# Eight adds of 128 spread through the statistics, in place of two adds of 512

## The chip, the core and the metric

The kernel runs on one core of one Trainium2 chip. A core has five engines that run their own instruction streams and meet only at semaphores: TensorE (PE, matmul and transpose; its weight loads are shown as PEld), VectorE (DVE), ScalarE (ACT), GpSimd (POOL) and SyncE (SP, which here only issues DMA). The metric is the device time of one execution in microseconds (us); lower is better.

## What is computed

One pre-normalised layer of a graph network: N = 50000 nodes of 128 features, E = 25000 edges with 32 features, all float32. The edges come sorted by their end node `dst`.

```python
h = jnp.maximum(_layernorm(x, axis=-1), 0.0)
src = edge_index[0]
dst = edge_index[1]
msg_input = jnp.concatenate([h[src], h[dst], edge_attr], axis=-1)
x = jax.nn.relu(msg_input @ Wm1 + bm1)
messages = jax.nn.relu(x @ Wm2 + bm2)
agg = jax.ops.segment_sum(messages, dst, num_segments=N)
update_input = jnp.concatenate([h, agg], axis=-1)
u = jax.nn.relu(update_input @ Wu1 + bu1)
h_new = h + (u @ Wu2 + bu2)
...
x = x + h_new
```

## The kernel before

The program has two parts with a barrier between them. Part one (to about 683 us in the profile) is a loop of 49 rounds, one for each block of 512 edges and 1024 nodes. Part two adds the messages up by node and makes the output. The change is in part one, in VectorE's program (`vector_1`).

A tile is 128 rows by 128 features. In round s part one takes 8 tiles of edge ends (4 of `x[src]`, 4 of `x[dst]`), gathered by GpSimd into `xg`, and 8 tiles of nodes, loaded into `xn` by a DMA that ScalarE issues. It forms the normalised edge ends, sends them through the two message layers, and leaves the messages in `msgs`. From the nodes it forms W_uh h + b_u1 (part of the update's first layer, `hu`) and x + h + b_out (`xh`). Both go to scratch in DRAM (`hu_scratch`, `xh_scratch`, 512 KB a round each), and part two reads them back.

The rounds are software-pipelined. Body s of VectorE does, in this order:

- waits until `xn` of round s has landed (L387), then the sixteen-column arithmetic of the layer norm of round s-1 (`statistics`, L312 to L355): `pair`, `diff`, `sq`, `mean`, `var`, `veps`, then, once ScalarE has made the square root `sd`, the reciprocal, a Newton step (r1, r2), `rstd` and `shift`. Each of these small instructions waits on a semaphore for the one before, and in the gaps `between(i)` puts independent work: `bn_stats` of node tile i of round s for i = 0 to 7 (L304), `x_plus_h` for i = 8 and 9 (L360, 512 wide: max(zn, 0) + xn of round s-2 into `xh_o`), `add_b_out` for i = 10 and 11 (L366, 512 wide);
- `normalise` of round s-1 (L378): the 8 tiles of `xg` in place, and one node tile into `zn`. ScalarE makes the other seven node tiles (L429) as soon as `shift` is there;
- waits for the gather of round s (L307) and takes `bn_stats` of its 8 tiles (L309).

ScalarE's round is, in program order: `sd` (L453); the bias eviction of the second W_uh product of round s-3 (L441); the first message layer's ReLU (L458); the bias eviction of the first W_uh product of round s-2 (L441, it waits for TensorE's L511); three `zn` tiles, which wait for `shift`; the issue of the two scratch stores of round s-3 (L447 `hu`, L449 `xh`); the second message layer's ReLU (L467); four `zn` tiles; the ReLU evictions of transposed groups 0 and 1 (L436); the issue of the load of `xn` and `edge` of round s+1 (L174, L181); the message eviction (L478); the evictions of groups 2 and 3, which also wait until both stores of this round have landed (L483). The stores and the loads share ScalarE's DMA queue and stand in it in that order.

TensorE's round is: W_uh product 0, second message layer, W_uh product 1, transposes of group 0 and 1 (the `xg` tiles, L504), message products (L534), transposes of groups 2 and 3 (`zn`), first message layer of the next round (L520 to L522).

GpSimd only gathers: it copies eight columns of indices, waits until the gather before has landed (L239), and issues eight indirect DMAs (L246). A slot of `xg` is free again three rounds later (L236).

`x_plus_h` and `add_b_out` count in `s_xs` and `s_xh`, each twice a round. Before it writes `xh_o`, VectorE waits that ScalarE and it itself have made `zn` of that round (`s_za`, `s_zv`), and that the stores that read this half of `xh_o` two rounds ago have landed (`s_sto`, L396).

Of the kernel before, what the change touches and what calls it, by code (L numbers as in the profile page):

```python
# [10 lines left out]
ALU = mybir.AluOpType  # L11
# [4 lines left out]
N, E, D, DE = 50000, 25000, 128, 32  # L16
# [26 lines left out]
def at_least(s, k):  # L43

    return not isinstance(s, int) or s >= k


def below(s, k):

    return not isinstance(s, int) or s < k  # L50


def build(nc, x, ends, dst_rows, dst_cols, edge_t, wm1, bm1, wm2, bm2, wu1, bu1, wu2, bu2, out):
    with ExitStack() as ctx:
        def sb(name, shape, dt=F32, on=ctx):
            return on.enter_context(nc.sbuf_tensor(name, shape, dt))
# [4 lines left out]
        def sem(name):  # L61
            return ctx.enter_context(nc.semaphore(name))
# [21 lines left out]
        xh_o = sb("xh_o", [P, 2, 2, W])  # L84
# [15 lines left out]
        s_xs, s_xh = sem("x_and_h_summed"), sem("xh_ready")  # L100
# [32 lines left out]
        with ExitStack() as one:  # L133
# [14 lines left out]
            xn = sb("xn", [P, 4, 8, D], on=one)  # L148
            zn = sb("zn", [P, 2, 8, D], on=one)
# [141 lines left out]
            def vector_1(dve):  # L291
# [20 lines left out]
                def statistics(s, slot, between):  # L312


                    half = slot % 2
                    if at_least(s, 2):
                        dve.wait_ge(s_za, 2 * (s - 1))
                        dve.wait_ge(s_zv, 3 * (s - 1))
                    dve.wait_ge(s_stat, STAT * s + 1)
                    dve.tensor_tensor(pair[:], bn[:, half, :, 1:3], bn[:, half, :, 4:6], ALU.add).then_inc(s_stat, 1)  # L320
                    dve.tensor_tensor(diff[:], bn[:, half, :, 1], bn[:, half, :, 4], ALU.subtract).then_inc(s_stat, 1)
                    between(0)
                    dve.wait_ge(s_stat, STAT * s + 3)
                    dve.scalar_tensor_tensor(out=sq[:], in0=diff[:], scalar=0.25, in1=diff[:], op0=ALU.mult,
                                             op1=ALU.mult).then_inc(s_stat, 1)
                    dve.tensor_scalar(mean[:, half], pair[:, :, 0], 0.5, None, ALU.mult).then_inc(s_stat, 1)
                    between(1)
                    dve.wait_ge(s_stat, STAT * s + 5)
                    dve.scalar_tensor_tensor(out=var[:], in0=pair[:, :, 1], scalar=1.0 / D, in1=sq[:], op0=ALU.mult,
                                             op1=ALU.add).then_inc(s_stat, 1)  # L330
                    between(2)
                    dve.wait_ge(s_stat, STAT * s + 6)
                    dve.tensor_scalar(veps[:], var[:], EPS, None, ALU.add).then_inc(s_stat, 1)  # L333
                    for i in range(3, 6):
                        between(i)
                    dve.wait_ge(s_sd, s + 1)
                    dve.reciprocal(r0[:], sd[:]).then_inc(s_stat, 1)
                    between(6)
                    dve.wait_ge(s_stat, STAT * s + 8)

                    dve.scalar_tensor_tensor(out=r1[:], in0=r0[:], scalar=-0.5, in1=r0[:], op0=ALU.mult,
                                             op1=ALU.mult).then_inc(s_stat, 1)
                    between(7)
                    dve.wait_ge(s_stat, STAT * s + 9)
                    dve.tensor_tensor(r2[:], r1[:], veps[:], ALU.mult).then_inc(s_stat, 1)
                    between(8)
                    dve.wait_ge(s_stat, STAT * s + 10)
                    dve.scalar_tensor_tensor(out=rstd[:, half], in0=r2[:], scalar=1.5, in1=r0[:], op0=ALU.add,  # L348
                                             op1=ALU.mult).then_inc(s_stat, 1)
                    between(9)  # L350
                    dve.wait_ge(s_stat, STAT * s + 11)
                    dve.scalar_tensor_tensor(out=shift[:, half], in0=mean[:, half], scalar=-1.0, in1=rstd[:, half], op0=ALU.mult,
                                             op1=ALU.mult).then_inc(s_stat, 1)
                    between(10)
                    between(11)  # L355

                def x_plus_h(s, slot, h):

                    half = slot % 2
                    dve.scalar_tensor_tensor(  # L360
                        out=xh_o[:, half, h, :].rearrange("p (j d) -> p j d", j=4), in0=zn[:, half, 4 * h:4 * h + 4, :],
                        scalar=0.0, in1=xn[:, slot, 4 * h:4 * h + 4, :], op0=ALU.max, op1=ALU.add).then_inc(s_xs, 1)

                def add_b_out(s, slot, h):
                    dve.wait_ge(s_xs, 2 * s + h + 1)
                    dve.tensor_tensor(xh_o[:, slot % 2, h, :], xh_o[:, slot % 2, h, :], b_out[:], ALU.add  # L366
                                      ).then_inc(s_xh, 1)
# [15 lines left out]
                def body(s, slot, use):  # L383
                    prev, prev2 = (slot - 1) % 4, (slot - 2) % 4
                    if below(s, STEPS):

                        dve.wait_ge(s_xn[slot], 32 * use + 32 + (0 if below(s, STEPS - 1) else 16))  # L387
                    def between(i):
                        if i < 8 and below(s, STEPS):
                            stat_of_nodes(s, slot, i)  # L390
                        if i == 8 and at_least(s, 2):
                            dve.wait_ge(s_za, 2 * (s - 1))
                            dve.wait_ge(s_zv, 3 * (s - 1))
                            if at_least(s, 4):

                                dve.wait_ge(s_sto[slot % 2], 64 * use + (32 if slot >= 2 else 0) - 32)  # L396
                        if i in (8, 9) and at_least(s, 2):
                            x_plus_h(s - 2, prev2, i - 8)
                        if i >= 10 and at_least(s, 2):
                            if not at_least(s, 3):  # L400
                                dve.wait_ge(s_w, 16 * 11)
                            add_b_out(s - 2, prev2, i - 10)

                    if at_least(s, 1) and below(s, STEPS + 1):
                        statistics(s - 1, prev, between)
                        normalise(s - 1, prev)
                    else:
                        for i in range(12):
                            between(i)
                    if not at_least(s, 1):  # L410
                        finish_table(dve, did)
                        assert steps[0] == TABLE
                    if below(s, STEPS):
                        stat_of_ends(s, slot, use)

                run_steps(dve, STEPS + 2, 4, STEPS - 1, 4, body)

            def scalar_1(act):
# [441 lines left out]
```

## Time and profile before

| | us |
|---|---|
| median of 3 runs | 946.89 |
| lowest, highest | 946.84, 947.41 |
| the profiled execution | 952.33 |
| its span on the core | 950.6 |

The rows further down come from that one profiled execution; its span is the time from its first to its last recorded instruction. In a timeline row the first number is the start, the second the time that the instruction (or the row of merged instructions, xN) is busy, and the bracket tells how long the engine sat idle before it and what released it. Instructions on VectorE and ScalarE overlap in their pipelines, so the distance between two starts is shorter than a row's busy time.

### The profile page before, as it was taken

To read this page: it belongs to the slowest core of one execution; us is meant where nothing else is said; L and a number is where in the kernel's file an instruction comes from. 1 tells how busy PE (TensorE), PEld (TensorE's weight loads), DVE (VectorE), ACT (ScalarE), POOL (GpSimd) and SP (SyncE) were. 2 spreads that over 40 slices of the span, in tenths; PEclk is the share of its full clock that TensorE was granted. 3 is DMA by queue.
4 is the path that set the end of the run, shared out by engine and by line. 5 is a ranking of instruction groups with operands and counts; after the bars stand their busy time and mean duration, and the time that the engine had idled before them with its cause. 6 is when DMAs were issued, how large, how long until landed. Compare 5 with 4: busy or idle time off the path is not lost. (4 is left out here: it accounts for less than half of the span.)

```text
span 950.6 us, 19507 instructions
## 1 busy us (share of the span) xinstructions
PE 751.0 (79%) x3158; PEld 453.1 (48%) x3159; DVE 696.0 (73%) x2407; ACT 608.5 (64%) x1384; POOL 566.0 (60%) x829
## 2 busy tenths in 40 slices
PE   0687768767877778877887776886799999999998
PEld 0344334333433334433443433453457788777776
DVE  3866756666677666776667567766499999998887
ACT  0666556556656565665665566655567788988986
POOL 6656655656566555665556555654198766655453
PEclk9988888889789897889887899988899999999999
DMA  6254445445545455545553454447305799999999
GB/s 158 67 178 158 151 154 175 157 127 178 176 157 168 141 176 165 169 148 161 177 176 129 153 176 155 162 150 232 133 12 176 230 319 335 351 341 349 355 360 328
DMA packets 99726, 184.55 MB, mean 194 GB/s; under 512 B 15101, under 2 KB 16512, under 8 KB 99700
## 3 DMA queue, kind: packets, MB, share of 16 engines
q1 hardware_dynamic: 46084, 80.64, 25.4%
q10 hardware_dynamic: 41072, 77.93, 23.5%
q0 software_dynamic: 12544, 25.72, 10.5%
q14 instruction: 20, 0.16, 0.1%
q8 instruction: 6, 0.10, 0.0%
HBM read 107.25 MB, written 76.98 MB: 194 GB/s over the span
## 5 line engine op out<-in xcount | busy, mean ns | idle before, releaser
L246 POOL DMA_INDIRECT xg<-x_in,ends_now x392 | 386.1, 985 | 142.9 <-issue 130.1
L511 PE MATMUL bank<-ht,w_uh 128*128 128x512 f32 x196 | 146.1, 837 | 114.2 <-ACT ht L441 68.8
L644 POOL TENSOR_TENSOR low<-msgs,high 128x128 fp32r<-128x128 f32 x303 | 152.8, 521 | 73.3 <-ACT high L724 70.1
L309 DVE BATCH_NORM_STATS2 bn<-xg 128x6 f32<-128x128 f32 x392 | 80.6, 278 | 132.4 <-DMA xg<-x_in,ends_now 132.3
L673 DVE TENSOR_SCALAR hot<-node,dst_f,minus_base 128x512 fp32r<-128x512 f32 x229 | 131.2, 616 | 23.2 <-issue 16.3
L777 PE MATMUL bank<-hot,low 128*128 128x512 f32 x303 | 136.4, 450 | 12.2 <-POOL low L644 6.5
L429 ACT ACTIVATE zn<-xn,shift,rstd 128x128 f32<-128x128 f32 x343 | 141.6, 483 | 1.6 <-DVE rstd L348 1.2
L511 PEld LDWEIGHTS bank<-ht,w_uh 128*128 128x128 f32 x196 | 42.6, 249 | 199.6 <-issue 180.1
L436 ACT ACTIVATE ht<-bank 128x512 f32<-128x512 f32 x196 | 109.2, 593 | 30.3 <-PE bank L504 26.1
L778 PE MATMUL bank<-hot,high 128*128 128x512 f32 x303 | 120.8, 399 | 0.0
L504 PE MATMUL bank<-ident,xg 128*128 128x128 f32 x392 | 64.8, 298 | 61.1 <-issue 37.0
L378 DVE TENSOR_SCALAR xg<-xg,mean,rstd 128x128 f32<-128x128 f32 x392 | 106.3, 352 | 0.0
L811 PEld LDWEIGHTS bank<-w_out,u_t 128*128 128x128 f32 x784 | 99.3, 191 | 14.2 <-issue 8.0
L811 PE MATMUL bank<-w_out,u_t 128*128 128x128 f32 x784 | 105.1, 277 | 0.2 <-ACT u_t L757 0.2
L441 ACT ACTIVATE ht<-bank,b_u 128x512 f32<-128x512 f32 x98 | 66.6, 680 | 58.5 <-issue 31.5
L504 PEld LDWEIGHTS bank<-ident,xg 128*128 128x128 f32 x392 | 49.0, 154 | 109.5 <-issue 90.7
L724 ACT ACTIVATE high<-msgs 128x128 fp32r x303 | 81.7, 298 | 28.6 <-issue 16.8
L304 DVE BATCH_NORM_STATS2 bn<-xn 128x6 f32<-128x128 f32 x392 | 98.3, 276 | 0.0
L453 ACT ACTIVATE sd<-veps 128x16 f32<-128x16 f32 x49 | 10.6, 216 | 125.6 <-DVE veps L333 102.8
L777 PEld LDWEIGHTS bank<-hot,low 128*128 128x128 f32 x303 | 57.9, 191 | 52.3 <-issue 25.3
L243 POOL COPY ends_now<-ends_all 128x8 int32 (+1 forms) x45 | 8.4, 187 | 115.5 <-DMA xg<-x_in,ends_now 56.8
L527 PE MATMUL bank<-m1t,w_msg 128*128 128x512 f32 x98 | 76.2, 873 | 0.0
(77 smaller groups left out, 1165.7 us busy)
## 6 DMA issues: line engine op xcount, KB each, us to landing
hu_scratch<-ht ACTq DMA_DIRECT2D x49, 512.0 KB
xh_scratch<-xh_o ACTq DMA_DIRECT2D x49, 512.0 KB
hu_i<-hu_scratch SPq DMA_DIRECT2D x98, 256.0 KB
xh_i<-xh_scratch SPq DMA_DIRECT2D x98, 256.0 KB
out<-xh_o SPq DMA_DIRECT2D x97, 256.0 KB, 4.3
xn<-x_in ACTq DMA_DIRECT2D x44, 512.0 KB
xg<-x_in,ends_now POOLq DMA_INDIRECT x392
edge<-edge_t_in ACTq DMA_DIRECT2D x45, 64.0 KB
```

What stands on the lines that cost most here:

```text
L246: pool.indirect_dma_start(xg[:, slot, t, :], None, x, bass.IndirectOffsetOnAxis(ap=ends_now[:, slot8, t:t + 1], axis=0)).then_inc(s_xg[slo ...
L304: dve.bn_stats(bn[:, slot % 2, 8 + t, :], xn[:, slot, t, :])
L378: ins = dve.tensor_scalar(to, of, mean[:, slot % 2, t:t + 1], rstd[:, slot % 2, t:t + 1], ALU.subtract, ALU.mult)
L429: ins = act.activation(zn[:, prev % 2, t - 8, :], xn[:, prev, t - 8, :], ACT.Identity, bias=shift[:, prev % 2, t:t + 1], scale=rstd[:, pre ...
L436: act.activation(ht[:, prev % 2, q, :], p_tr[q][:], ACT.Relu).then_inc(s_ht, 1)
L504: ins = pe.transpose(p_tr[q][:, j * P:(j + 1) * P], of, ident[:])
L511: pe.matmul(p_hu[:], w_uh[:], ht[:, slot % 2, 2 + n, :], start=True, stop=True).then_inc(s_hus, 1)
L644: return pool.tensor_tensor(low[:, at, :], msgs[:, k, :], high[:, at, :].bitcast(F32), ALU.subtract)
L673: return dve.tensor_scalar(hot[:, at, :], node[:], dst_f[:, bass.ds(k, 1)], minus_base[:, bass.ds(g, 1)], ALU.subtract, ALU.is_equal)
L777: pe.matmul(to, low[:, at, :], hot[:, at, :], start=start, stop=False, skip_group_check=True)
L778: return pe.matmul(to, high[:, at, :], hot[:, at, :], start=False, stop=stop, skip_group_check=True)
L811: ins = pe.matmul(to[:, j * D:(j + 1) * D], u_t[:, slot % 2, j * P:(j + 1) * P], w_out[:], start=True, stop=True)
```

## The change

`x_plus_h` is cut from two instructions of 512 columns a round to eight of 128, one behind each `bn_stats` of the node tiles. The three waits ahead of it move with it, from before position 8 to position 0. Only the fourth and the eighth of the eight add one to `s_xs`, so that there are still two increments a round. `add_b_out` stays 512 wide and moves from positions 10 and 11, behind `shift`, to positions 8 and 9: one between r2 and `rstd`, one between `rstd` and `shift`.

```diff
                     dve.scalar_tensor_tensor(out=shift[:, half], in0=mean[:, half], scalar=-1.0, in1=rstd[:, half], op0=ALU.mult,
                                              op1=ALU.mult).then_inc(s_stat, 1)
-                    between(10)
-                    between(11)
-
-                def x_plus_h(s, slot, h):
-
-                    half = slot % 2
-                    dve.scalar_tensor_tensor(
-                        out=xh_o[:, half, h, :].rearrange("p (j d) -> p j d", j=4), in0=zn[:, half, 4 * h:4 * h + 4, :],
-                        scalar=0.0, in1=xn[:, slot, 4 * h:4 * h + 4, :], op0=ALU.max, op1=ALU.add).then_inc(s_xs, 1)
+
+                def x_plus_h(s, slot, t):
+
+                    ins = dve.scalar_tensor_tensor(
+                        out=xh_o[:, slot % 2, t // 4, t % 4 * D:(t % 4 + 1) * D], in0=zn[:, slot % 2, t, :],
+                        scalar=0.0, in1=xn[:, slot, t, :], op0=ALU.max, op1=ALU.add)
+                    if t % 4 == 3:
+                        ins.then_inc(s_xs, 1)
...
-                        if i == 8 and at_least(s, 2):
+                        if i == 0 and at_least(s, 2):
                             dve.wait_ge(s_za, 2 * (s - 1))
                             dve.wait_ge(s_zv, 3 * (s - 1))
                             if at_least(s, 4):
 
                                 dve.wait_ge(s_sto[slot % 2], 64 * use + (32 if slot >= 2 else 0) - 32)
+                        if i < 8 and at_least(s, 2):
+                            x_plus_h(s - 2, prev2, i)
                         if i in (8, 9) and at_least(s, 2):
-                            x_plus_h(s - 2, prev2, i - 8)
-                        if i >= 10 and at_least(s, 2):
                             if not at_least(s, 3):
                                 dve.wait_ge(s_w, 16 * 11)
-                            add_b_out(s - 2, prev2, i - 10)
+                            add_b_out(s - 2, prev2, i - 8)
```

On VectorE, in a round ahead of the loop, between `var` and the reciprocal (L337). `sd` is made by ScalarE from `veps`. Before:

```order
L329 SCALAR_TENSOR_TENSOR var<-pair,sq 128x16
L304 BN_STATS bn<-xn 128x6
L333 TENSOR_SCALAR veps<-var 128x16
L304 BN_STATS bn<-xn 128x6 x3
L337 RECIPROCAL r<-sd 128x16
```

And now:

```order
L329 SCALAR_TENSOR_TENSOR var<-pair,sq 128x16
L304 BN_STATS bn<-xn 128x6
L357 SCALAR_TENSOR_TENSOR xh_o<-zn,xn 128x128
L333 TENSOR_SCALAR veps<-var 128x16
L304 BN_STATS bn<-xn 128x6
L357 SCALAR_TENSOR_TENSOR xh_o<-zn,xn 128x128
L304 BN_STATS bn<-xn 128x6
L357 SCALAR_TENSOR_TENSOR xh_o<-zn,xn 128x128
L304 BN_STATS bn<-xn 128x6
L357 SCALAR_TENSOR_TENSOR xh_o<-zn,xn 128x128
L337 RECIPROCAL r<-sd 128x16
```

One narrow add stands behind each `bn_stats`; three of the eight are ahead of `veps`, three more ahead of the reciprocal.

On VectorE, in the same round, from the last Newton product (`r<-r,veps`) to the normalisation of the gathered tiles. Before:

```order
L345 TENSOR_TENSOR r<-r,veps 128x16
L360 SCALAR_TENSOR_TENSOR xh_o<-zn,xn 128x512
L348 SCALAR_TENSOR_TENSOR rstd<-r 128x16
L360 SCALAR_TENSOR_TENSOR xh_o<-zn,xn 128x512
L352 SCALAR_TENSOR_TENSOR shift<-mean,rstd 128x16
L366 TENSOR_TENSOR xh_o<-xh_o,b_out 128x512 x2
L378 TENSOR_SCALAR xg<-xg,mean,rstd 128x128 x8
```

And now:

```order
L345 TENSOR_TENSOR r<-r,veps 128x16
L365 TENSOR_TENSOR xh_o<-xh_o,b_out 128x512
L348 SCALAR_TENSOR_TENSOR rstd<-r 128x16
L365 TENSOR_TENSOR xh_o<-xh_o,b_out 128x512
L352 SCALAR_TENSOR_TENSOR shift<-mean,rstd 128x16
L377 TENSOR_SCALAR xg<-xg,mean,rstd 128x128 x8
L377 TENSOR_SCALAR zn<-xn,mean,rstd 128x128
```

The two wide adds of `b_out` took the places of the two wide `x_plus_h`, so that nothing stands between `shift` and the normalisation any more. No other engine's order is changed.

## Rows read from the trace of the kernel before

**Rows 1.** Waits by engine and line, 100 to 640 us: total, times, longest.
```profile
DVE bn L309 <- DMA xg<-x_in,ends_now: 115.3, 40, 5.8
...
DVE pair L320 <- DMA edge<-edge_t_in: 58.0, 33, 2.6
```

**Rows 2.** Timeline of VectorE: `pair` that opens body 3 and, 44 rounds later, body 47.
```profile
45.15 0.20 DVE L320 TENSOR_TENSOR pair<-bn 128x32 f32<-128x32 f32 x1
...
637.07 0.20 DVE L320 TENSOR_TENSOR pair<-bn 128x32 f32<-128x32 f32 x1 [1.99 <-DMA edge<-edge_t_in]
```

**Rows 3.** Timeline of VectorE, one round, 301.31 to 315.00 us, and the next one's end.
```profile
301.31 0.19 DVE L320 TENSOR_TENSOR pair<-bn 128x32 f32<-128x32 f32 x1 [1.39 <-DMA edge<-edge_t_in]
...
301.72 0.16 DVE L324 SCALAR_TENSOR_TENSOR sq<-diff 128x16 f32<-128x16 f32 x1
301.81 0.16 DVE L326 TENSOR_SCALAR mean<-pair 128x16 f32<-128x16 f32 x1
...
302.43 0.66 DVE L304 BATCH_NORM_STATS2 bn<-xn 128x6 f32<-128x128 f32 x3
...
303.76 0.69 DVE L360 SCALAR_TENSOR_TENSOR xh_o<-zn,xn 128x512 f32<-128x512 f32 x1
...
305.06 0.17 DVE L352 SCALAR_TENSOR_TENSOR shift<-mean,rstd 128x16 f32<-128x16 f32 x1
...
306.35 2.13 DVE L378 TENSOR_SCALAR xg<-xg,mean,rstd 128x128 f32<-128x128 f32 x8
...
310.89 1.64 DVE L309 BATCH_NORM_STATS2 bn<-xg 128x6 f32<-128x128 f32 x8 [2.15 <-DMA xg<-x_in,ends_now]
315.00 0.20 DVE L320 TENSOR_TENSOR pair<-bn 128x32 f32<-128x32 f32 x1 [2.46 <-DMA edge<-edge_t_in]
...
328.04 0.20 DVE L320 TENSOR_TENSOR pair<-bn 128x32 f32<-128x32 f32 x1 [1.58 <-DMA edge<-edge_t_in]
```

**Rows 4.** Timeline of ScalarE and its DMA issues (ACTq), the same round and the next.
```profile
305.31 0.48 ACT L429 ACTIVATE zn<-xn,shift,rstd 128x128 f32<-128x128 f32 x1
...
305.95 0.42 ACTq L449 DMA_DIRECT2D xh_scratch<-xh_o  x1
...
310.50 0.60 ACT L436 ACTIVATE ht<-bank 128x512 f32<-128x512 f32 x1 [1.35 <-PE bank L504]
310.73 0.40 ACTq L174 DMA_DIRECT2D xn<-x_in  x1
...
319.83 0.48 ACT L429 ACTIVATE zn<-xn,shift,rstd 128x128 f32<-128x128 f32 x1
320.20 0.42 ACTq L449 DMA_DIRECT2D xh_scratch<-xh_o  x1
...
324.05 0.40 ACTq L174 DMA_DIRECT2D xn<-x_in  x1
```

**Rows 5.** Timeline of TensorE, the transposes of group 1 in that round.
```profile
308.54 0.66 PE L504 MATMUL bank<-ident,xg 128*128 128x128 f32 x4 [0.30 <-issue]
```

**Rows 6.** Stretches: engines' busy us, granted clock (PEclk), DMA share, GB/s.
```profile
305.95:310.30 4.35, 3.12 (x22) 2.18 (x21) 2.79 (x10) 3.20 (x8) 2.74 (x3) 1.00 0.90 300
315.00:320.00 5.00, 2.84 (x4) 1.17 (x4) 4.98 (x23) 2.12 (x5) 3.78 (x5) 0.55 0.20 54
```

**Rows 7.** Timeline of GpSimd, the copies that open two of its rounds.
```profile
311.09 0.19 POOL L243 COPY ends_now<-ends_all 128x8 int32 x1 [1.79 <-PE bank L504]
...
325.04 0.19 POOL L243 COPY ends_now<-ends_all 128x8 int32 x1 [3.44 <-DMA xg<-x_in,ends_now]
```

**Rows 8.** Timeline, a round with a late gather, from its `pair`.
```profile
111.67 0.20 DVE L320 TENSOR_TENSOR pair<-bn 128x32 f32<-128x32 f32 x1 [0.17 <-DVE bn L309]
...
116.76 0.42 ACTq L449 DMA_DIRECT2D xh_scratch<-xh_o  x1
...
119.89 0.40 ACTq L174 DMA_DIRECT2D xn<-x_in  x1
...
125.00 1.64 DVE L309 BATCH_NORM_STATS2 bn<-xg 128x6 f32<-128x128 f32 x8 [5.82 <-DMA xg<-x_in,ends_now]
```

More of the change, by code:

```diff
@@ L407, in body @@
                     else:
-                        for i in range(12):
+                        for i in range(10):
                             between(i)
```

## The prediction

> **What bounds the kernel now.** I read the waits first: VectorE waits in every round for the gathered tiles (115.3 us in 40 waits between 100 and 640 us) and in most again, at `pair`, for the load of the nodes (58.0 us in 33) [rows 1]. A total does not say which of the two sets the pace, so I read rounds in the timeline. From `pair` at 45.15 to `pair` at 637.07 there are 44 rounds of 13.45 us on average [rows 2]. In the round from 301.31 the gather lands at 310.89, its statistics take 1.64 us, and VectorE then sits 2.46 us until the load is there, at 315.00 [rows 3]. The wait that ends last is the one for the load; the gather has over 2 us of slack. So one round is a ring: `pair`, statistics, normalisation, transposes, eviction of group 1, issue of the next load (L174, 9.42 us after `pair`), its landing (4.27 us), next `pair`: 13.69 us. The next round has 9.05 and 3.99 us, 13.04 in all [rows 3, 4].
>
> Two kinds of round alternate irregularly. In the round from 301.31 the granted clock is 1.00 (2.4 GHz) from the stores' issue to their end. In the first 5 us of the next it is 0.55 on average, mostly the lower level of 1.2 GHz [rows 6], TensorE's W_uh products take longer there, and the first `zn` follows `pair` by 4.83 us in place of 4.00 [rows 3, 4]. About half of the rounds are of each kind.
>
> GpSimd has a ring of its own: copy, eight gathers, landing, copy. Between two copies lie 13.95 us, 3.44 of them idle; with the 1.79 us of idle that another round has, it would be 12.3 us [rows 7]. It is the faster ring, by about 1 us. In five of 47 rounds it nevertheless decides: the load is issued 3.13 us after the stores (4.78 in the round above), the gather lands only at 125.00, 13.33 us after `pair`, and with its statistics of 1.64 the round takes 15.0 us [rows 3, 4, 8].
>
> **The narrow add.** Only starts count, since instructions overlap. A 16-column instruction of this kind takes 0.09 us (`sq` to `mean`). The 512-column one takes 0.61: from 303.76 to 305.06 there are two and one `rstd`, (1.30 - 0.09)/2. A line through both gives 0.09 + 0.52 x 112/496 = 0.207 us at 128 columns, and eight `bn_stats` of 128 columns in a row take 1.64 us, 0.205 each [rows 3]. Eight take 1.65 us in place of 1.21: **+0.44 us** a round. The other end is 0.27 us, that of a tile of the `xg` normalisation with its two column operands (2.13/8) [rows 3]: +0.92. I take 0.207, as both nearest rows agree. No gap of the statistics chain is there to swallow it: from `pair` to `shift`, 3.75 us, VectorE's rows carry no idle time in brackets [rows 3]. So the interleaving hides nothing; below zero is excluded.
>
> One rule speaks for a higher price. Three narrow instructions in a row are recorded as 0.66 us together, and a wide one as 0.69 though the next wide one follows it closely [rows 3]: they overlap. The Trainium skill (VectorE: DVE Perf Modes, the section on the TRN2 errata) says that the latency is exposed between instructions, so that many small tiles pay it each time, and gives (N+151)/0.96 for an fp32 add; by that, as an estimate, eight of 128 take 2.33 us and two of 512 1.38, +0.95 a round, in place of +0.44. The trace agrees with its duration of 0.69 for one of 512 columns, not with paying it in full between instructions.
>
> **The moved adds of b_out.** Their two 0.6 us are spent either way (from `shift` at 305.06 to the normalisation at 306.35: 1.29, less 0.09, is 1.20 for two) [rows 3]. But they now come ahead of `shift`. `shift` moves from 3.75 us after `pair` to 3.75 + 0.44 + 1.20 = 5.39. Three paths lead from `pair` to the issue of the load:
> - VectorE's own: the normalisation of `xg`, from which group 1 is transposed, starts 0.44 later. In rounds at full clock this path decides: ScalarE waits 1.35 us for group 1 [rows 4]. **+0.44**.
> - `veps` and `sd`: three narrow adds now stand ahead of `veps`, 0.62 us. `sd` and all that ScalarE does behind it, the evictions that TensorE's W_uh products wait for among them, come 0.6 later. In rounds at low clock TensorE reaches the transposes late by this path. **+0.6**.
> - ScalarE's `zn` tiles: they start 0.25 us behind `shift` (305.06 to 305.31), so at 5.6 us, where they were at 4.0 and 4.83. From the first to the issue of the load are 4.22 us in the round with little waiting (319.83 to 324.05) [rows 3, 4]; 5.6 + 4.2 = 9.8, against 9.42 + 0.44 = 9.86 and 9.05 + 0.6 = 9.65. So this path becomes level with the others and adds 0 to 0.15. I take 0.
>
> The mean of 0.44 and 0.60 is +0.52 a round.
>
> **The stores.** They are issued behind the third `zn`, 4.64 and 5.20 us after `pair` (L449); 0.64 behind the first `zn`, they go to about 6.25 [rows 3, 4]. They keep the DMA 0.90 busy for 4.35 us [rows 6], now until 10.6 us. The load, issued at 9.8 behind them in the same queue, has 3.55 us from the stores' issue in place of 4.78 and 3.85. With 3.85 it landed as fast (3.99 us) as with 4.78 (4.27), with 3.13 the round was late by the gather [rows 4, 8]. The load's landing thus costs 0 to 0.8 us more (its queue ahead ends 0.8 after its issue); I take 0, the distance being nearer to 3.85. But late rounds become more frequent: each costs 15.0 - 13.3 = 1.7 us, and I count two more, **+3 us** in all.
>
> **The waits that move.** `s_za` and `s_zv` were satisfied in the round before. `s_sto` asks for the stores of the round before, and VectorE has just waited for a load that stands behind them in the queue; it can bind only in the last body, where no load is waited for, and there the same two stages of work stand behind it as before. Two increments a round stay two. Part two is untouched.
>
> **Sum.** 47 rounds end in a wait for a load, 47 x 0.52 = 24.4 us; the two bodies behind them have only VectorE's 0.44 each, 0.9; late rounds 3. Together +28 us on the profiled 952.33, which is 980.6, or 1.030. On the median of 946.89 that is **975 us**. With 0.44 everywhere and no late rounds it is 967; with 0.6 + 0.15 a round and four late ones 990.
>
> **Rivals.**
> - *Absorbed.* If the gathers really set the pace, VectorE's longer work only shortens its 2.15 us wait for them: 947. For it: that wait is the larger total [rows 1]. Against: the wait for the load follows it and ends last in most rounds [rows 3].
> - *Faster.* The five late rounds vanish because the slower main ring leaves the gather ring more slack, while the +0.44 hides in the 1.35 us for which group 1's signal is late: its transposes are recorded at 308.54 for 0.66 us, yet ScalarE gets it at 310.50 [rows 4, 5]. Then 5 x 1.6 = 8 us are gained: 939. It decides once the signal does not move with VectorE. Against: low-clock rounds show no such gap.
> - *Stores, gathers and load collide in most rounds.* The load now follows the stores at 3.55 us, between the 3.13 of a late round and 3.85. If half of the rounds take 15 us [rows 8], the mean gains (15.0 - 13.3)/2 = 0.85, and the other half keeps its share of 0.52, 0.26; together +1.11, 47 x 1.11 = 52: 999.
> - *The late signal belongs to the store burst.* Group 1's signal at 310.50 coincides with the end of the burst at 310.30 [rows 4, 6]. If the burst holds it, the load moves by as much as the stores, 1.6 and 1.05 us: 47 x 1.3 = 61: 1008.
> - *The narrow adds cost +0.92* (their upper end): 0.96 or so a round with the rest, 45 + 3: 995. The skill's page named above gives nearly the same price.
>
> **Chances.** Forecast 0.58; absorbed 0.10; faster 0.07; collisions 0.15; burst 0.06; dear adds 0.04. The two rivals below my forecast are the 0.17 that I leave out, with part of the burst case: range 957 to 1000. A measurement of this kernel tells about 0.2% from no change: faster by more 0.08, within it 0.09, slower 0.83.
>
> **What would show it.** Right: narrow adds start about 0.2 us apart; `shift` at 5.4 us behind `pair`; the first L428 `zn` at 5.6 and the stores' issue at 6.2; the load's issue at 9.7 to 9.9, landing about 4 us later; mean round 14.0. VectorE's wait at `pair` for the load stays or grows, that for the gather shrinks by less than 0.5. Wrong: a round that stays at 13.4 (the gathers' ring), a load issue near 11 us (the burst), or rounds of 15 with waits of over 5 us for the gather in more than a fourth of all (collisions).

## The result and the profile after

The changed kernel takes 980.52 us (median of 4 runs, 977.82 to 985.02) against 947.15 (4 runs). The ratio is 1.0356, with a 95% interval of 1.0316 to 1.0395: slower, by 33 us where 28 were forecast. The profiled execution has a span of 978.4 us, 950.6 before: 28 us more and not 33, since the profiled execution of the kernel before (952.33) is itself 5 us above the median. These 28 us all lie in part one: from the third body's `pair` on, 42 rounds take 14.15 us each in place of 13.47.

VectorE's timeline of the changed kernel, `pair` of body 3 and, 42 rounds later, of body 45 (start, busy us, engine, line, operation; in brackets the idle time before it and its releaser), which answers to [rows 2]:

```profile
44.47 0.20 DVE L320 TENSOR_TENSOR pair<-bn 128x32 f32<-128x32 f32 x1
...
638.78 0.20 DVE L320 TENSOR_TENSOR pair<-bn 128x32 f32<-128x32 f32 x1 [4.35 <-DMA edge<-edge_t_in]
```

Its waits between 100 and 640 us (total, times, longest), which answer to [rows 1]:

```profile
DVE pair L320 <- DMA edge<-edge_t_in: 174.6, 38, 5.3
...
ACT msgs L477 <- remote: 100.0, 35, 4.2
...
DVE bn L309 <- DMA xg<-x_in,ends_now: 2.7, 1, 2.7
```

VectorE waits no longer for the gathers (115.3 us before, 2.7 now) and three times as long for the load (58.0 before, 174.6 now). That the load's ring sets the pace was right; but the gathers now have a lead: they have landed before VectorE asks for them, which no step of mine foresaw.

One round on VectorE, beside [rows 3]:

```profile
314.95 0.20 DVE L320 TENSOR_TENSOR pair<-bn 128x32 f32<-128x32 f32 x1 [4.89 <-DMA edge<-edge_t_in]
...
316.19 0.29 DVE L304 BATCH_NORM_STATS2 bn<-xn 128x6 f32<-128x128 f32 x1
316.40 0.28 DVE L357 SCALAR_TENSOR_TENSOR xh_o<-zn,xn 128x128 f32<-128x128 f32 x1
316.59 0.17 DVE L333 TENSOR_SCALAR veps<-var 128x16 f32<-128x16 f32 x1
...
320.21 0.17 DVE L352 SCALAR_TENSOR_TENSOR shift<-mean,rstd 128x16 f32<-128x16 f32 x1
...
322.65 1.64 DVE L309 BATCH_NORM_STATS2 bn<-xg 128x6 f32<-128x128 f32 x8
328.84 0.20 DVE L320 TENSOR_TENSOR pair<-bn 128x32 f32<-128x32 f32 x1 [4.56 <-DMA edge<-edge_t_in]
```

A narrow add takes 0.19 us from its start to the next (0.207 forecast). `shift` stands 5.26 us behind `pair` (5.39 forecast, 3.75 before). The statistics of the gathered tiles follow the normalisation with no wait at all, and 4.56 us of idle time come at the end.

ScalarE in the same round, beside [rows 4]:

```profile
316.79 0.21 ACT L452 ACTIVATE sd<-veps 128x16 f32<-128x16 f32 x1 [1.66 <-DVE veps L333]
...
320.41 0.49 ACT L428 ACTIVATE zn<-xn,shift,rstd 128x128 f32<-128x128 f32 x1
...
321.10 0.43 ACTq L448 DMA_DIRECT2D xh_scratch<-xh_o  x1
...
324.48 0.40 ACTq L174 DMA_DIRECT2D xn<-x_in  x1
...
327.76 0.60 ACT L477 ACTIVATE msgs<-bank 128x512 f32 x1 [2.85 <-remote]
```

The first `zn` starts 5.46 us after `pair` and the stores are issued at 6.15 (5.6 and 6.25 forecast). The load is issued at 9.53 in this round and at 9.08 on average. That is no later than before (9.14), where 9.7 to 9.9 was forecast. It lands 4.36 us later here and 5.07 on average, against 4.33 before. So the issue did not move; the landing did.

Why the issue did not move shows on ScalarE. Before, it idled ahead of the evictions of the transposed groups (waits from 100 to 640 us, the kernel before):

```profile
ACT ht L436 <- PE bank L504: 23.1, 31, 1.9
```

Over the 42 rounds that is 0.59 us a round ahead of groups 0 and 1. In the changed kernel it is 0.05: VectorE's later work and the later `zn` tiles went into a wait that had been there. And from the first `zn` to the load's issue are 3.51 us on average (5.57 to 9.08), where 4.22 was forecast. A round at full clock of the changed kernel, its `pair` at 582.48:

```profile
587.94 0.49 ACT L428 ACTIVATE zn<-xn,shift,rstd 128x128 f32<-128x128 f32 x1 [0.86 <-DVE shift L352]
...
588.63 0.42 ACTq L448 DMA_DIRECT2D xh_scratch<-xh_o  x1
...
590.93 0.40 ACTq L174 DMA_DIRECT2D xn<-x_in  x1
```

Here the load is issued 8.45 us after `pair`, over 1 us earlier than in the round from 314.95, with the stores at the same 6.15. The round is no shorter for it: 13.85 us against 13.89.

The share of the DMA engines fits this. Stretches of 1 us of the kernel before, the round of [rows 3] (busy us of the engines, granted clock, DMA share, GB/s):

```profile
308.31:309.31 1.00, 0.77 (x7) 0.77 (x8) 0.43 (x2) 0.84 (x2) 0.98 (x1) 1.00 1.02 356
309.31:310.31 1.00, 1.00 (x11) 1.00 (x11) 0.00 (x0) 0.00 (x0) 0.00 (x0) 1.00 0.71 189
310.31:311.31 1.00, 0.81 (x7) 0.58 (x6) 0.42 (x3) 0.60 (x1) 0.19 (x1) 1.00 0.02 4
311.31:312.31 1.00, 1.00 (x3) 0.52 (x4) 1.00 (x7) 0.52 (x2) 0.54 (x1) 1.00 0.44 68
312.31:313.31 1.00, 1.00 (x3) 0.24 (x2) 0.23 (x2) 1.00 (x3) 0.70 (x2) 1.00 0.97 342
```

And of the changed kernel, from its stores on:

```profile
321.95:322.95 1.00, 1.00 (x2) 0.23 (x1) 1.00 (x5) 1.00 (x4) 0.69 (x2) 0.50 1.02 350
322.95:323.95 1.00, 1.00 (x9) 0.97 (x8) 1.00 (x6) 0.98 (x4) 0.69 (x2) 0.78 1.04 402
323.95:324.95 1.00, 1.00 (x11) 1.00 (x10) 0.33 (x2) 0.96 (x2) 0.90 (x1) 1.00 0.97 301
324.95:325.95 1.00, 1.00 (x11) 1.00 (x10) 0.00 (x0) 0.00 (x0) 0.79 (x1) 1.00 0.78 113
325.95:326.95 1.00, 1.00 (x4) 0.45 (x3) 0.00 (x0) 0.00 (x0) 0.16 (x1) 1.00 0.71 258
326.95:327.95 1.00, 1.00 (x3) 0.29 (x2) 0.00 (x0) 0.19 (x1) 0.00 (x0) 1.00 1.00 377
```

Before, the DMA engines fall idle (0.02) between the stores and the load: the load waits for its issue. Now stores, gathered rows (the second at 0.78 and only 113 GB/s) and load follow each other without a gap: the load waits for what is ahead of it. Its landing follows the stores' issue, 7.7 us earlier in this round and 7.9 on average (14.15 - 6.25), and no longer its own. The rounds of the timeline agree: in the 41 that end in this wait, the load lands the slower the closer it is issued behind the `xh` store (slope -0.96, correlation -0.89). In 34 such rounds of the kernel before the slope is 0.04.

### The profile page after: what moved, and what is told of

It reads as the page before. It is cut to its first block and busy times, and to the rows that moved or that the text cites. A ratio compares the mean times of both kernels' runs of the same rounds, so it can differ in the third digit from the quotient of the medians.

```text
span 978.4 us, 19801 instructions
## 1 busy us (share of the span) xinstructions
PE 766.3 (78%) x3158; PEld 459.7 (47%) x3159; DVE 710.2 (73%) x2701; ACT 608.0 (62%) x1384; POOL 572.0 (58%) x829
## 5 line engine op out<-in xcount | busy, mean ns | idle before, releaser
L510 PE MATMUL bank<-ht,w_uh 128*128 128x512 f32 x196 | 164.0, 933 | 158.0 <-ACT ht L440 143.1
L510 PEld LDWEIGHTS bank<-ht,w_uh 128*128 128x128 f32 x196 | 48.4, 275 | 247.3 <-issue 196.8
L320 DVE TENSOR_TENSOR pair<-bn 128x32 f32<-128x32 f32 x49 | 9.6, 196 | 197.6 <-DMA edge<-edge_t_in 192.2
L304 DVE BATCH_NORM_STATS2 bn<-xn 128x6 f32<-128x128 f32 x392 | 108.2, 278 | 0.0
L357 DVE SCALAR_TENSOR_TENSOR xh_o<-zn,xn 128x128 f32<-128x128 f32 x392 | 105.6, 271 | 3.4 <-DMA xh_scratch<-xh_o 3.4
L477 ACT ACTIVATE msgs<-bank 128x512 f32 (+1 forms) x49 | 29.2, 597 | 113.0 <-remote 107.0
L503 PEld LDWEIGHTS bank<-ident,xg 128*128 128x128 f32 x392 | 52.2, 158 | 82.3 <-issue 77.6
L503 PE MATMUL bank<-ident,xg 128*128 128x128 f32 x392 | 59.6, 294 | 35.1 <-issue 30.2
L526 PE MATMUL bank<-m1t,w_msg 128*128 128x512 f32 x98 | 86.7, 985 | 0.0
```

Source lines behind the costliest of these rows:

```text
L304: dve.bn_stats(bn[:, slot % 2, 8 + t, :], xn[:, slot, t, :])
L503: ins = pe.transpose(p_tr[q][:, j * P:(j + 1) * P], of, ident[:])
L510: pe.matmul(p_hu[:], w_uh[:], ht[:, slot % 2, 2 + n, :], start=True, stop=True).then_inc(s_hus, 1)
```

## The experiments

I formed two theories from this. The **path theory** is my prediction's: the round grows because the narrow adds and `sd` make the load's issue late. The **store theory**: `shift` holds the first `zn` tiles, behind them the stores, and the load lands about 8 us behind the stores' issue. The table gives, for each kernel, the ratio to the kernel before on the same chip with its 95% interval, and means over the same 42 rounds of the profiled execution, taken from the timelines' rows: the round, `shift`, the issue of the `xh` store and of the load (us after `pair`), and VectorE's wait for the gathers. Each mean is of one execution: that of the kernel before is 0.6% above its median, that of "before, stores early" 0.6% below (933.61 against 939.0), so differences of 0.1 us between rounds say nothing, and the ratios decide.

| kernel | ratio (95%) | round | shift | stores | load | gather wait |
|---|---|---|---|---|---|---|
| before | 1 | 13.47 | 3.79 | 4.99 | 9.14 | 2.95 |
| changed | 1.0356 (1.0316 to 1.0395) | 14.15 | 5.33 | 6.25 | 9.08 | 0.36 |
| only narrowed | 1.0046 (1.002 to 1.0072) | 13.52 | 4.29 | 5.34 | 8.98 | 0.30 |
| adds behind shift | 1.0183 (1.0132 to 1.0233) | 13.74 | 4.40 | 5.69 | 9.33 | 0.19 |
| narrow adds behind root | 1.0345 (1.0279 to 1.0411) | 14.22 | 5.42 | 6.33 | 8.87 | 0.18 |
| before, stores late | 1.0311 (1.0228 to 1.0395) | 14.13 | 3.79 | 6.11 | 9.30 | 4.25 |
| changed, stores ahead of zn | 1.0195 (1.0149 to 1.0241) | 13.69 | 5.42 | 5.45 | 9.31 | 0.22 |
| changed, loads by SyncE | 1.0277 (1.0205 to 1.0350) | 13.72 | 5.28 | 6.17 | 9.54 | 3.33 |
| changed, stores early | 1.0271 (1.0221 to 1.0320) | 13.85 | 5.38 | 3.42 | 9.51 | 0.06 |
| before, stores early | 0.9970 (0.9941 to 1.0000) | 13.12 | 3.80 | 2.76 | 8.93 | 0.46 |
| wide adds ahead of shift | 1.0605 (1.0558 to 1.0652) | 14.62 | 4.87 | 5.78 | 8.70 | 5.22 |
| before, load at head | 0.9698 (0.9656 to 0.9740) | 12.59 | 3.77 | 4.83 | (11.47) | 3.45 |
| changed, load at head | 0.9864 (0.9814 to 0.9914) | 13.05 | 5.27 | 6.18 | (11.65) | 3.60 |
| before, load at head, stores early | 0.9663 (0.9623 to 0.9703) | 12.65 | 3.78 | 2.80 | (11.65) | 3.51 |

(In brackets: with the load at the head of ScalarE's body, the issue that falls into the round is that of a load which is needed only a round later.)

### Only narrowed

```diff
                         if i in (8, 9) and at_least(s, 2):
-                            x_plus_h(s - 2, prev2, i - 8)
+                            for t in range(4 * (i - 8), 4 * (i - 8) + 4):
+                                x_plus_h(s - 2, prev2, t)
```

> The kernel before with nothing but the narrowing: four narrow adds at each of the two old places (8 and 9), b_out behind shift. The disputed cost by itself. VectorE takes 0.44 us more a round, shift comes at 4.2, the first zn at 4.4 (full clock) or 4.85 (low), the stores' issue at 5.1 to 5.2. Path theory: 47 x 0.44 = 21 us, 968. Store theory: the stores are later by 0.4 in full-clock rounds alone and not late enough to bind (5.2 + 8.0 = 13.2), so only what VectorE's path gives in full-clock rounds: 950 to 962.

1.0046, some 4 us. It is clear of no change but far from 21 us. `shift` came at 4.29, half a microsecond later than before (0.44 forecast), and the stores at 5.34. This kernel's gathers run ahead too (its wait for them is 0.30 us a round), so the few late rounds of [rows 8] are gone, and part of the price may be paid back by that; this was not separated.

### The two moved parts, each without the other

The adds of `b_out` back behind `shift`, the narrow ones spread as in the change:

```diff
-                        if i in (8, 9) and at_least(s, 2):
+                        if i >= 10 and at_least(s, 2):
...
-                            add_b_out(s - 2, prev2, i - 8)
+                            add_b_out(s - 2, prev2, i - 10)
```

> The changed kernel with the two wide adds of b_out back behind shift; the eight narrow adds stay spread through the statistics. Store theory (the load lands about 8 us after the stores' issue, because it queues behind them): shift goes back to about 4.1 us after pair, but sd is still 0.6 late, so in rounds at low clock the first zn and the stores' issue stay at 5.45 and 6.15 and only the rounds at full clock get their stores at about 5.3; mean round 13.8 to 14.0, 965 to 975 us. Path theory (my prediction's: VectorE's own path and sd's path to the load's issue): the moved adds cost nothing by themselves, so as the changed kernel, 978 to 983. If shift alone is what delays the stores: near 955.

All narrow adds behind the reciprocal, the adds of `b_out` ahead of `shift`:

```diff
-                        if i == 0 and at_least(s, 2):
+                        if i == 6 and at_least(s, 2):
...
-                        if i < 8 and at_least(s, 2):
-                            x_plus_h(s - 2, prev2, i)
+                        if i in (6, 7) and at_least(s, 2):
+                            for t in range(4 * (i - 6), 4 * (i - 6) + 4):
+                                x_plus_h(s - 2, prev2, t)
```

> The changed kernel with all eight narrow adds behind the reciprocal (four at position 6, four at 7), so that veps and sd are as early as in the kernel before; the adds of b_out stay ahead of shift, at 5.3 us after pair. Store theory: first zn at 5.5 and stores' issue at 6.15 in every round, since shift alone holds them: as the changed kernel, mean round 14.1, 976 to 983. Path theory: the 0.6 us of the low-clock rounds is gone and only VectorE's 0.44 is left: 965 to 970.

With `shift` early and `sd` late: 1.0183, 13.74 us a round (963 us, just under what the store theory gave). With `shift` late and `sd` early: 1.0345, the whole loss, 14.22. Beside the narrowing alone (1.0046), spreading the adds ahead of `sd` costs 1.4% and moving the `b_out` adds ahead of `shift` 3.0%; together they cost 3.1%, not 4.4%. They don't add up because the first `zn` starts at the later of two events: at 4.79 us on average with the narrowing alone, 5.29 and 5.63 in these two, 5.57 in the changed kernel. There both stand at the same time: the eviction of the W_uh product, late by `sd`, lets it start at 5.46 in rounds at the low clock, and `shift` lets it start at 5.46 in the others. The path theory, which made `sd` half of the loss and the `b_out` adds free, is refuted in this: 965 to 970 was expected of the second kernel and 979 to 982 came.

### Stores late, VectorE untouched

```diff
-                    if at_least(s, 3):
-                        store(s - 3, (slot + 1) % 2)
...
                         normalise(range(12, 16))
+                    if at_least(s, 3):
+                        store(s - 3, (slot + 1) % 2)
```

> The kernel before, VectorE untouched, with ScalarE's two stores issued behind the second four zn in place of the first three: their issue goes from 4.6 to 5.2 to about 7.3 to 8.1 us after pair, and nothing that makes the load's issue late is touched. Store theory: the load lands 8 us behind the stores' issue, rounds of 15.3 to 16: 1030 to 1065. Path theory: the load's issue at 9.2 and its landing in 4.0 are unchanged, up to 0.8 more for the queue: 947 to 985.

Nothing on VectorE differs from the kernel before and the load's issue hardly moves (9.30), yet the round is 14.13 us and the ratio 1.0311. The direction is the store theory's, and the size is near the loss of the change. The size I had expected (1030 us and more) was wrong for one reason first: ScalarE's queue issues DMAs while the `zn` tiles ahead of them still run, so the stores went out at 6.11 on average and not at 7.3 to 8.1. One of its rounds, VectorE and ScalarE's issues:

```profile
256.99 0.19 DVE L320 TENSOR_TENSOR pair<-bn 128x32 f32<-128x32 f32 x1 [0.91 <-DMA edge<-edge_t_in]
...
268.68 1.64 DVE L309 BATCH_NORM_STATS2 bn<-xg 128x6 f32<-128x128 f32 x8 [4.27 <-DMA xg<-x_in,ends_now]
270.70 0.20 DVE L320 TENSOR_TENSOR pair<-bn 128x32 f32<-128x32 f32 x1 [0.38 <-DMA edge<-edge_t_in]
```

```profile
263.64 0.42 ACTq L449 DMA_DIRECT2D xh_scratch<-xh_o  x1
...
266.34 0.40 ACTq L174 DMA_DIRECT2D xn<-x_in  x1
```

Stores at 6.65, load at 9.35, landing at 13.71, only 7.1 us behind the stores; the gather lands 11.69 us after `pair`, close ahead of the load. In other rounds of this kernel the gather is the later of the two (VectorE waits 4.25 us a round for it). So later stores alone, with VectorE untouched, bring a loss of that size; they hold both the load and the gathers, and 8 us is no constant.

### Taking the stores out of the way of the changed kernel

Three ways. Ahead of the `zn` tiles, so that they don't wait for `shift`:

```diff
+                    if at_least(s, 3):
+                        store(s - 3, (slot + 1) % 2)
                     if has_norm:
                         act.wait_ge(s_stat, STAT * (s - 1) + 12)
                         normalise(range(VECTOR_TILES, 12))
-                    if at_least(s, 3):
-                        store(s - 3, (slot + 1) % 2)
```

> The changed kernel with ScalarE's two stores issued ahead of the first zn tiles, so that they no longer stand behind the wait for shift; VectorE as changed. Store theory: the stores' issue comes back to 4.5 (full clock) or 5.3 (low), mean round 13.4 to 13.6, 945 to 958. Path theory: the load's issue is late by VectorE and sd as before and the stores don't matter: 975 to 981.

Right behind the eviction that they need:

```diff
                         w_h(s - 3, (slot - 3) % 2, 1)
+                        store(s - 3, (slot + 1) % 2)
```

> The changed kernel with the stores issued right behind the eviction of W_uh product 1, so at about 3.3 us after pair whatever shift does. Store theory: all that is left of the change is VectorE's 0.44 and sd's 0.6 on the way to the load's issue; a ratio of 0.997 (the kernel before with early stores) to 1.015. Path theory: the ratio stays at 1.03 and above.

And the load through SyncE's queue, at the same point of the round:

```diff
+                def ahead(s, slot, use):
+                    if below(s, STEPS - 1) and at_least(s, 3):
+                        sp.wait_ge(s_ht, 4 * (s - 1) + 1)
+                        sp.wait_ge(s_tr, 4 * (s - 1) + 2)
+                        sp.wait_ge(s_xh, 2 * (s - 2))
+                        sp.wait_ge(s_m1, s - 2)
+                        load_nodes(sp, s + 1, (slot + 1) % 4)
...
-                    if below(s, STEPS - 1) and at_least(s, 3):
-                        act.wait_ge(s_xh, 2 * (s - 2))
-                        act.wait_ge(s_m1, s - 2)
-                        load_nodes(act, s + 1, (slot + 1) % 4)
```

> The changed kernel with the load of xn and edge issued by SyncE instead of ScalarE, at the same point of the round (group 0 evicted, group 1 transposed), so through another DMA queue. If the load is late because it stands behind the stores in one queue: it now shares the DMA engines with them and lands about 4 us after its issue at 9, mean round 13.3 to 13.7, 945 to 960. If the DMA engines' total work behind the stores (1 MB of stores, the gathers' rows, 0.5 MB of load) sets it and not the queue's order: 975 to 985.

They give 1.0195, 1.0271 and 1.0277, rounds of 13.69, 13.85 and 13.72 us. The last two don't differ clearly from each other, and SyncE's interval overlaps the change's. The three edits thus take back 0.8 to 1.6% of 3.6; none is back at the kernel before, as the store theory wanted, and the last two stay near the 3% of the path theory. What the stores cost the change can be more than was taken back, for the two moved issues bring waits of their own: ahead of the `zn` tiles they hold the first of these to 6.16 us (5.57 in the changed kernel), and early they hold the first layer's ReLU, 44.1 us in 38 waits:

```profile
ACT m1t L458 <- issue: 44.1, 38, 1.3
```

Through SyncE's queue the load is issued at 9.54 and lands 4.2 us later, not 5.07. That speaks for its place behind the stores in one queue, but the gathers have no lead in that kernel, so it is no clean comparison.

In the kernel with early stores the load no longer lands late, and the way to its issue is what is left. A round of it:

```profile
285.35 0.20 DVE L320 TENSOR_TENSOR pair<-bn 128x32 f32<-128x32 f32 x1 [4.48 <-DMA edge<-edge_t_in]
...
290.62 0.18 DVE L352 SCALAR_TENSOR_TENSOR shift<-mean,rstd 128x16 f32<-128x16 f32 x1
...
298.71 0.19 DVE L320 TENSOR_TENSOR pair<-bn 128x32 f32<-128x32 f32 x1 [4.00 <-DMA edge<-edge_t_in]
```

```profile
288.66 0.42 ACTq L448 DMA_DIRECT2D xh_scratch<-xh_o  x1
290.84 1.26 ACT L428 ACTIVATE zn<-xn,shift,rstd 128x128 f32<-128x128 f32 x3 [0.44 <-DVE shift L352]
...
294.57 0.40 ACTq L174 DMA_DIRECT2D xn<-x_in  x1
```

The stores are out at 3.31, ScalarE waits for `shift`, the load is issued at 9.22 and lands 4.14 us later. That kernel's partner is the kernel before with the same edit, whose first ReLU waits as long (48.8 us in 42 waits):

> The kernel before with the stores issued right behind the eviction of W_uh product 1 that they need, about 2 us after pair instead of 4.6 to 5.2. Store theory: the burst is over at 7, group 1's signal isn't held by it, the load is issued at 8.2 to 9 and lands in 4: rounds of 12.4 to 13.0, 897 to 926. Path theory: nothing on the path moves, 940 to 950.

It is at 0.9970, rounds of 13.12 and a load issue at 8.93. Early stores alone bring the kernel before hardly anything: the 12.4 to 13.0 that the store theory gave was missed. And between the two kernels with early stores the change costs 1.0271/0.9970 = 1.030, its load issue going from 8.93 to 9.51, +0.58 us (+0.46 without the first five rounds, in four of which `shift` came up to 1.5 us late). There the path theory has the size (+0.52 forecast). It has not the way: ScalarE waits only 0.05 us a round for the transposes, which leaves ScalarE's own tiles behind `shift`, the path that I had priced at nothing.

### The adds of b_out ahead of shift, nothing narrowed

```diff
-                    between(10)
-                    between(11)
...
-                        if i in (8, 9) and at_least(s, 2):
-                            x_plus_h(s - 2, prev2, i - 8)
-                        if i >= 10 and at_least(s, 2):
+                        if i in (6, 7) and at_least(s, 2):
+                            x_plus_h(s - 2, prev2, i - 6)
+                        if i in (8, 9) and at_least(s, 2):
```

> The kernel before without any narrowing: the two wide x_plus_h at positions 6 and 7 (behind the reciprocal), the two adds of b_out at 8 and 9, ahead of shift. The same work on VectorE as before, sd as early as before, only shift is later: 4.95 us after pair, first zn at 5.2, stores' issue at 5.9. Store theory: mean round 13.8 to 14.0, a ratio of 1.017 to 1.027. If the narrow adds are needed for the loss: 1.000 to 1.005.

1.0605, the slowest of all, though VectorE does less than in the change and `shift` comes earlier (4.87). Neither theory had this. Its timeline, VectorE and ScalarE's issues:

```profile
364.47 0.20 DVE L320 TENSOR_TENSOR pair<-bn 128x32 f32<-128x32 f32 x1
...
378.03 1.65 DVE L309 BATCH_NORM_STATS2 bn<-xg 128x6 f32<-128x128 f32 x8 [6.20 <-DMA xg<-x_in,ends_now]
379.71 0.20 DVE L320 TENSOR_TENSOR pair<-bn 128x32 f32<-128x32 f32 x1
```

```profile
370.20 0.42 ACTq L447 DMA_DIRECT2D xh_scratch<-xh_o  x1
...
372.80 0.40 ACTq L174 DMA_DIRECT2D xn<-x_in  x1
```

This is the late round of [rows 8]: the load is issued 2.60 us behind the stores, the gather lands 13.56 us after `pair`, and the round is 15.24 us. 28 of the 42 rounds take over 14.4 us in this kernel, six before. It is my rival of stores, gathers and load that collide, at full strength. In the changed kernel it did not come about: there the gathers have their lead and VectorE does not wait for them.

The lead is there in every kernel with narrow adds whose loads ScalarE issues in the old place: the wait for the gathers is nil from the eighth body on at the latest. The kernel before with early stores nearly has the lead as well (0.46 us a round). In the changed kernel the rounds from `pair` at 115.18 and at 129.95 are long (14.77 and 15.08 us) and hold waits of VectorE for its own semaphores, and from the first of them on the gathers have their lead. In the kernel before, the one with late stores and the one with wide adds ahead of `shift` they never gain it. What decides whether the lead is gained stays open. None of the runs changed the gathers' lead alone, so that it keeps the collisions away is argued, not shown.

### The load out of the ring

The buffer for the next load is free at the start of ScalarE's body, so the load can be issued there:

```diff
+                    if below(s, STEPS - 1) and at_least(s, 3):
+                        act.wait_ge(s_xh, 2 * (s - 2))
+                        act.wait_ge(s_m1, s - 2)
+                        load_nodes(act, s + 1, (slot + 1) % 4)
                     if has_norm:
                         act.wait_ge(s_stat, STAT * (s - 1) + 7)
```

> The kernel before with the load of the next round issued at the head of ScalarE's body (its buffer is free by then), ahead of the stores. The wait for the load leaves the ring. Both theories: the round is then set by the gathers' ring (12.3 us and more, as its rows are also served beside the stores) or by TensorE and ScalarE: 12.4 to 13.2 a round, 900 to 935. If instead GpSimd's ring is what set 13.45 all along: 947.

0.9698: 912.92 us against 941.1 on that chip. Its only wait of weight on VectorE between 100 and 640 us:

```profile
DVE bn L309 <- DMA xg<-x_in,ends_now: 144.9, 42, 5.2
```

The wait at `pair` is gone, and the gathers' ring sets the round: 12.59 us, where [rows 7] gave 12.3. The changed kernel with the same edit:

> The changed kernel with the load of the next round at the head of ScalarE's body. With the load out of the ring the gathers' ring decides, and VectorE waits 3.4 us for it. If the change acts through the load alone: as the kernel before with the load at the head, ratio 0.965 to 0.975. If the later stores also hold the last gathers' landing: rounds of 12.75 to 13.2, 0.975 to 1.00.

0.9864, so the change still costs 1.7% (13.05 against 12.59 us). VectorE has 3.6 us of slack to the gathers, which hides 0.44 us of its work. What is left is that the gather lands later after `pair` (11.37 against 10.91), which is the round's whole 0.46 us. That fits stores that go out 1.35 us later beside the last gathers, but no run separated it. Both edits on the kernel before:

> The kernel before with both: the load at the head of ScalarE's body and the stores right behind the eviction of product 1. The burst is over before the last gathers are issued, so the gathers' ring should run at its 12.3 us: ratio 0.955 to 0.970. If load and stores so close together hold the gathers instead: 0.975 or more.

0.9663 (0.9623 to 0.9703), not to be told apart from 0.9698. Either version is about 3% faster than the kernel before and 6% faster than the changed one.

## Where the prediction was right and where not

- **Sign and size**: 975 forecast, 980.5 measured (on a kernel before of 947.15), inside 957 to 1000. Faster and absorbed are refuted.
- **What bounds the kernel**: right. The load's ring sets the round, since taking the load out of it gains 3%, and the gathers' ring stands right behind (12.6 us).
- **The narrow add at 0.207 us, `shift` at 5.39, `zn` at 5.6, stores at 6.25**: measured 0.19, 5.26, 5.46 and 6.15 in the round shown. The dear adds of the rival did not come. By the Trainium skill's rule (VectorE: DVE Perf Modes, the section on the TRN2 errata), by which each small tile pays the latency, `shift` would have come another 0.5 us later, an estimate from the page's figures; the measurement decides against it for instructions that follow each other like these.
- **+0.44 for VectorE's own path**: VectorE's work grew by about as much (0.50), but as a price of its own it was too high, 4 us measured for the narrowing where 21 were counted. That this path decides in the rounds at full clock was wrong for the changed kernel: ScalarE's wait for group 1, on which it rested, is nearly gone there (0.05 us a round).
- **"This path becomes level with the others", the moved `b_out` adds at 0 to 0.15**: wrong as a share. They are the largest part, 3.0% on top of the narrowing, and 6.05% without it, where the gathers collide. The path from the first `zn` was computed to be level with the others; it took 3.51 us instead of 4.22 and still set the load's issue. That the stores behind these tiles matter was priced at nothing but the late rounds.
- **"The load's landing costs 0 to 0.8 us more; I take 0"**: the step that failed. The landing grew by 0.74 us (5.07 against 4.33), and the load's issue, forecast 0.5 to 0.7 us later, did not move. The two errors have nearly the same size and opposite sign, so that the sum came out well by luck as much as by method. In the kernels with early stores the issue moved about as forecast (+0.58).
- **Late rounds, +3 us**: the stretch between the stores' issue and the load's shrank, to 2.83 us where 3.55 was computed. Yet none of the changed kernel's rounds waits over 3.5 us for a gather, so this term did not come as it was meant, while such waits filled the kernel with wide adds. The count of five such rounds before was low as well: in the kernel before seven of the 42 rounds end without a wait for the load, two of them not long.
- **The waits that move**: right but for one body. `s_sto` ahead of the first narrow add costs 3.4 us in two bodies, the last ones of part one, where it cost 1.7 in one before:

```profile
DVE xh_o L357 <- DMA xh_scratch<-xh_o: 3.4, 2, 2.4
```

## What to carry to other kernels

An operation that is moved out of the tail of one engine's chain into its middle is not moved for nothing: whatever hangs on the chain's end comes later, and on another engine that can be the issue of a DMA which other DMAs queue behind. When a round is set by a load, look for what stands between the buffer's release and the load's issue before tuning the arithmetic; here one moved issue gained 3%, and each rearrangement of the arithmetic that was measured cost between 0.5 and 6%. A burst, a load and small gathers that follow each other closely have more than one steady pattern, so a forecast made from one pattern can be right in sum and wrong in its terms.

## What the runs showed of the hardware that I had not expected

- ScalarE's queue issues a DMA that stands behind computing instructions before these have run: in the kernel with late stores the `xh` store, behind seven `zn` tiles in program order, is issued at 263.64 us, while the last three of them start at 263.94:

```profile
263.94 1.25 ACT L429 ACTIVATE zn<-xn,shift,rstd 128x128 f32<-128x128 f32 x3
```

- A consumer can start long after its producer's recorded end while the DMA engines are busy. In the changed kernel TensorE's message products are recorded from 324.06 to 325.12, and ScalarE starts their eviction only at 327.76 after 2.85 us of waiting, when the load's data are in; over 35 rounds this is 100.0 us of waiting. It lies off the ring. The cause stays unsettled: the ends of matmuls are modelled in the trace, and with the loads issued by SyncE the same wait has 6.8 us behind `remote` and 3.8 behind TensorE, so it may belong to ScalarE's own DMA issues as well as to a late signal.

```profile
324.06 1.06 PE L533 MATMUL bank<-w_ua,m2t 128*128 128x128 f32 x8
```

- The granted clock of TensorE fell from a mean of 0.908 to 0.878 with the longer rounds. Two rounds of the changed kernel, one at a mean of 0.80 from `pair` to the stores and one at 0.63, are as long as each other (13.85 and 13.89 us), so the clock is not shown to be a part of the loss:

```profile
582.48:588.60 6.12, 3.35 (x5) 1.41 (x6) 6.12 (x33) 2.77 (x7) 4.25 (x6) 0.80 0.12 32
```

```profile
314.95:321.10 6.15, 3.37 (x4) 1.46 (x5) 6.15 (x33) 2.84 (x7) 4.42 (x5) 0.63 0.12 32
```
